# Attention values by seven block products instead of eight, one step behind the scores

## The reference

```python
q = (inputs_q @ Wq).reshape(b, sq, H, HD) * (1.0 / np.sqrt(HD))     # H = 16 heads of 128
k = (inputs_kv @ Wk).reshape(b, skv, H, HD)                         # skv = 12544, D = 512
v = (inputs_kv @ Wv).reshape(b, skv, H, HD)
scores = jnp.einsum('bqhd,bkhd->bhqk', q, k)
attn = jax.nn.softmax(scores, axis=-1)
ctx = jnp.einsum('bhqk,bkhd->bqhd', attn, v).reshape(b, sq, H * HD)
return ctx @ Wo
```

## Time and profile before

| | |
|---|---|
| median of 3 runs | 2128.65 us (2127.99 to 2130.28) |
| time of the profiled execution | 2126.51 us |
| its span, first to last instruction | 2124.7 us |
| mean granted PE clock | 0.988 |
| PE busy | 2053.5 us, 97% of the span |
| DVE busy | 1197.5 us, 56% |
| ACT busy | 914.0 us, 43% |
| POOL busy | 152.0 us, 7% |

### The profile page before, as it was taken

The page is one execution under the profiler, slowest core; times in us unless marked ns, Lnnn a source line. Parts: engine busy times, 40 slices in busy tenths (PEclk is TensorE's granted clock), DMA queues, the critical chain, the costliest instruction groups (busy, mean ns, idle before and its releaser), DMA issues.

```text
span 2124.7 us, 29323 instructions
## 1 busy us (share of the span) xinstructions
PE 2053.5 (97%) x11196; PEld 1107.3 (52%) x11200; DVE 1197.5 (56%) x2159; ACT 914.0 (43%) x1985; POOL 152.0 (7%) x209
## 2 busy tenths in 40 slices
PE   5899999999999999999999999999999999999886
PEld 4645555555555455555555555555555555555562
DVE  5665555455555556665666665555545555554426
ACT  4444445444444444344444444444444444443212
POOL 1000100000100101001001001010010010000001
PEclk8899999999999999999999999999999999999998
DMA  5424535444445344454545553443434333423660
GB/s 165 119 58 87 109 80 120 83 106 99 99 90 114 65 100 104 103 119 89 128 95 112 110 102 75 90 89 66 100 65 90 74 86 75 95 60 55 189 222 5
DMA packets 516699, 206.75 MB, mean 97 GB/s; under 512 B 418864, under 2 KB 502832, under 8 KB 515664
## 3 DMA queue, kind: packets, MB, share of 16 engines
q1 hardware_dynamic: 516560, 204.88, 43.6%
HBM read 97.59 MB, written 4.46 MB: 48 GB/s over the span
## 4 chain that ended last, share of the span: by engine, by line
PE 92%; DVE 4%; issue 1%; DMA 1%; ACT 1%; POOL 1%; SPq 0%; DVEq 0%; POOLq 0%; ACTq 0%
PE ps_s L1102 24%; PE ps_t L1102 18%; PE ps_c L1126 12%; PE ps_b L1126 12%; PE ps_a L1126 12%; PE ps_u L1126 12%; PE ps_b L1080 1%; PE ps_t L1184 1%; DVE bulk L775 1%; DMA bulk<-in_vo 0%; PE ps_s L1063 0%; PE ps_s L1227 0%; POOL stages L498 0%; DVE unt L909 0%; PE ps_u L1251 0%
## 5 line engine op out<-in xcount | busy, mean ns | idle before, releaser
L1102 PE MATMUL ps_s<-bulk 128*128 128x384 f16 (+2 forms) x3264 | 579.5, 321 | 27.1 <-DVE bulk L775 26.2
L1102 PE MATMUL ps_t<-bulk 128*128 128x384 f16 (+2 forms) x2448 | 449.3, 320 | 1.3 <-ACT ps_t L628 1.0
L1102 PEld LDWEIGHTS ps_s<-bulk 128*128 128x128 f16 x3264 | 315.2, 98 | 241.3 <-DVE bulk L775 29.2
L1102 PEld LDWEIGHTS ps_t<-bulk 128*128 128x128 f16 x2448 | 235.0, 98 | 151.1 <-ACT ps_t L628 1.9
L628 ACT ACTIVATE ps_t<-ps_s 128x384 f32<-128x384 f32 (+2 forms) x136 | 62.9, 462 | 502.6 <-PE ps_s L1102 502.6
L1126 PE MATMUL ps_u<-nring,pt 128*128 128x512 f16 x1194 | 269.1, 379 | 0.0
L1126 PE MATMUL ps_a<-nring,pt 128*128 128x512 f16 x1194 | 269.1, 379 | 0.0
L498 POOL TENSOR_TENSOR stages<-stages 128x256 f32<-128x256 f32 x196 | 143.6, 732 | 1683.3 <-DMA stages<-in_ctx 1664.1
L1126 PE MATMUL ps_b<-nring,pt 128*128 128x512 f16 x1158 | 260.7, 379 | 0.0
L1126 PE MATMUL ps_c<-nring,pt 128*128 128x512 f16 x1158 | 260.7, 379 | 0.0
L808 DVE SCALAR_TENSOR_TENSOR pp<-prob,pp 128x768 f16<-128x768 f32 (+2 forms) x272 | 239.0, 920 | 0.0
(11 more groups left out here) (197 smaller groups left out, 1556.3 us busy)
## 6 DMA issues: line engine op xcount, KB each, us to landing
stages<-in_ctx SPq DMA_DIRECT2D x392, 128.0 KB, 2.8
wst<-in_w SPq DMA_DIRECT2D x64, 256.0 KB, 3.3
bulk<-in_vo SPq DMA_DIRECT2D x16, 512.0 KB, 4.7
acc<-in_qk SPq DMA_DIRECT2D x12, 512.0 KB, 5.1
pt<-pp SPq DMA_TRANSPOSE x272, 4.0
tern_d<-wter SPq DMA_DIRECT2D x32, 128.0 KB, 3.1
bulk<-tern_d SPq DMA_DIRECT2D x2, 2048.0 KB, 10.7
wst<-in_qk SPq DMA_DIRECT2D x4, 512.0 KB, 5.6
```

The source lines that it names most:

```text
L1102: ins = mm(out, q_part(e, qlo, a)[:, c * P:(c + 1) * P], t_moving(k, tlo, b, c), start=(first and c == 0 and qlo == 0 and tlo == 0), stop= ...
```

## The change

The values are now also a 2 x 2 block product of seven block products: the rows are the two heads, the inner halves are the two halves of a chunk, and the outer halves are the two halves of the 512 columns. Each block product has matmuls of 256 columns, three for each chunk.

- POOL forms four sums of probability blocks (`S1` to `S4`, each 128 x 384 float32 at w = 3) for each step, after the exponentials (`sum_p`). It also forms the four context sums for the value layout now (`sum_t` for both kinds of chunk).
- ACT and DVE make high and low parts of seven blocks instead of four: one piece of three blocks (A22, A11, A12), then S1, S3, S2, S4 one by one. S2 and S4 are done at the start of the next step.
- SP transposes seven blocks of high and low parts in two DMAs, group 0 with A22, A11, A12, S1 and group 1 with S2, S3, S4. `pt` is single buffered.
- The values run one step behind the scores (`LAG = 1`), with the copies `value_a`, `value_e_u` on ACT and the additions `value_sums` on DVE between their products.
- The value layout of a context chunk grows from 1024 to 1792 columns, in high and low parts.
- Buffers share memory: `diff`, `mask`, `wg1`, `wg2` are loaded near the end, `x` is loaded again at the end, and the last attention weight `aw_o` is loaded together with `aw_k` and `aw_v` instead of after the last head.
- In the first eight steps the query parts are made one step earlier, and the queries and the new value products use the same PSUM.

```diff
-LAG = 2
+LAG = 1
...
-P_SCALE = 2.0 ** 15
+P_SCALE = 2.0 ** 14
...
             def turn_p(k, g):
-                sp.wait_ge(lo_done[g], k + 1)
-                if k >= LAG:
-                    sp.wait_ge(u_done[g], k - 1)
-                n = 4 * cols(k)
-                at = ((k % 2) * 2 + g) * 4 * WIN * P
-                sp.dma_start_transpose(pt[:, at:at + n].rearrange("p (t q) -> p t q", q=P),
-                                       pp[:, g * 2 * WIN * BLK:g * 2 * WIN * BLK + n]).then_inc(in_pt[g], 16)
+                sp.wait_ge(lo_done, 5 * k + (2, 5)[g])
+                if k:
+                    sp.wait_ge(v4_done, k)
+                at, n = p_at(k, g), (8, 6)[g] * cols(k)
+                sp.dma_start_transpose(pt[:, at:at + n].rearrange("p (t q) -> p t q", q=P), pp[:, at:at + n]).then_inc(in_pt[g], 16)
...
             sp.wait_ge(s4_done, NS)
             sp.dma_start(aw_q, aw_d[0]).then_inc(in_aw, 16)
             load_vo(4)
-            sp.wait_ge(u_done[1], NS)
-            for n, w in enumerate((aw_k, aw_v)):
+            sp.wait_ge(v4_done, NS)
+            for n, w in enumerate((aw_k, aw_v, aw_o)):
                 sp.dma_start(w, aw_d[n + 1]).then_inc(in_aw2[n], 16)
-                load_vo(5 + 2 * n)
-                load_vo(6 + 2 * n)
+                load_vo(5 + n)
+            sp.dma_start(xin, x_d).then_inc(in_xr, 16)
+            load_vo(8)
...
+            def sum_p(k):
+                for n, (dst, a, b, op) in enumerate(((S1, A21, A22, ALU.add), (S3, A11, A21, ALU.subtract),
+                                                     (S2, S1, A11, ALU.subtract), (S4, A12, S2, ALU.subtract))):
+                    if n == 0:
+                        pool.wait_ge(exp_done[0], k + 1)
...
+                    if n == 1:
+                        pool.wait_ge(exp_done[1], k + 1)
+                    if n >= 2:
+                        pool.wait_ge(p_sum, 4 * k + n - 1 + (n == 3))
+                    nc.gpsimd.tensor_tensor(prob_part(k, dst), prob_part(k, a), prob_part(k, b), op).then_inc(p_sum, 1)
...
+            for k in range(NS):
+                found = prep_at(k)
+                if found is not None:
+                    sum_t(found[0])
+                sum_p(k)
...
+            def value_a(k):
+                act.wait_ge(v1_done, k + 1)
+                if k:
+                    act.wait_ge(acc_done[0], k)
+                nc.scalar.activation(val_b, val_a, ACT.Copy).then_inc(va_copied, 1)
+
+            def value_e_u(k):
+                act.wait_ge(v5_done, k + 1)
...
+                nc.scalar.activation(part_e[:, 0:BLK], val_e, ACT.Copy).then_inc(ve_copied, 1)
+                act.wait_ge(v6_done, k + 1)
...
+                nc.scalar.activation(part_u[:, 0:BLK], val_b, ACT.Copy).then_inc(vu_copied, 1)
...
             def step(k):      
                 nc.scalar.activation(bank_b(k), bank_a(k), ACT.Copy).then_inc(a_copied, 1)
+                if k:
+                    hi_part(k - 1, S2, 1, 3)
                 act.wait_ge(s5_done, k + 1)
                 nc.scalar.activation(part_e[:, 0:cols(k)], bank_e(k), ACT.Copy).then_inc(e_copied, 1)
+                if k:
+                    hi_part(k - 1, S4, 1, 4)
...
+                if k:
+                    value_a(k - 1)
                 exp_head(k, 0)
+                if k:
+                    value_e_u(k - 1)
                 exp_head(k, 1)
...
+                hi_part(k, A22, 3, 0)
+                hi_part(k, S1, 1, 1)
+                hi_part(k, S3, 1, 2)
...
+            def value_sums(k):                             # DVE
+                v.wait_ge(v7_done, k + 1)
...
+                nc.vector.tensor_tensor(val_d, val_b, part_e[:, 0:BLK], ALU.add).then_inc(vd_done, 1)
+                v.wait_ge(v3_done, k + 1)
+                v.wait_ge(vu_copied, k + 1)
+                nc.vector.tensor_tensor(val_e, val_e, part_u[:, 0:BLK], ALU.add).then_inc(ve_done, 1)
...
             def step(k):                                   # DVE
+                if k:
+                    lo_part(k - 1, S2, 1, 4)
+                add_values(k - 2, 1)
+                if k:
+                    lo_part(k - 1, S4, 1, 5)
+                add_values(k - 2, 0)
...
+                if k:
+                    value_sums(k - 1)
+                lo_part(k, A22, 3, 1)
+                lo_part(k, S1, 1, 2)
+                lo_part(k, S3, 1, 3)
...
+            def value_product(k, dst, a, b, first, last):
+                for n in range(w):
...
+                    for plo, clo in ((0, 0), (0, 1), (1, 0)):
+                        tile = p_at(k, g, plo, a % PURE) + n * P
+                        ins = mm(dst, pt[:, tile:tile + P], n_part(c, clo, b), start=(first and n == 0 and plo == 0 and clo == 0),
+                                 stop=(last and n == w - 1 and plo == 1), skip_group_check=True)
...
+            def values(k):
+                pe.wait_ge(in_pt[0], 16 * (k + 1))
...
+                if k:
+                    pe.wait_ge(acc_done[0], k)
+                    pe.wait_ge(acc_done[1], k)
...
+                value_product(k, val_a, A11, B11, True, False).then_inc(v1_done, 1)
...
+                value_product(k, val_e, S1, T1, True, False).then_inc(v5_done, 1)
+                pe.wait_ge(in_pt[1], 16 * (k + 1))
+                pe.wait_ge(va_copied, k + 1)
+                value_product(k, val_b, S2, T2, False, False).then_inc(v6_done, 1)
+                value_product(k, val_a, A12, B21, False, True)
+                pe.wait_ge(vu_copied, k + 1)
+                value_product(k, val_b, S3, T3, False, False).then_inc(v7_done, 1)
+                pe.wait_ge(ve_copied, k + 1)
+                value_product(k, val_e, S4, B22, False, True).then_inc(v3_done, 1)
+                pe.wait_ge(vd_done, k + 1)
+                value_product(k, val_b, A22, T4, False, True).then_inc(v4_done, 1)
```

More of the change, by code:

```diff
@@ L176, in perceiver_layer @@
         b2b, nwb = wst[:, 0:D], wst[:, D:2 * D]
-        aw_k, aw_v = (nring[:, n * KC * D:(n + 1) * KC * D] for n in range(2))
-        aw_o = unt[:, :]
+        aw_k, aw_v, aw_o = (nring[:, n * KC * D:(n + 1) * KC * D] for n in range(3))
+        xin, x1 = (nring[:, 3 * KC * D + n * D:3 * KC * D + (n + 1) * D] for n in range(2))
+        xin0, y0 = (pt[:, n * 2 * D:(n + 1) * 2 * D].bitcast(F32) for n in range(2))
         decay = stages[:, 0:AH * P]
+        late = stages[:, 8 * BLK:16 * BLK]
+        diff, mask, g1t, wg1 = (late[:, n * P:(n + 1) * P] for n in range(4))
+        wg2 = late[:, 4 * P:4 * P + D]
         xt = x2
@@ L590, in split_hi @@
                     return
[L591 removed]
+                j, kind, c = found
+                act.wait_ge(t_sum, 4 * (j + 1))
                 if kind == 0:
[L593 removed]
                     dst = t_ring(c, 0)
@@ L1132, in step @@
-            def step(k, between=None):
+            def value_product(k, dst, a, b, first, last):
+                _, lowest, w = STEPS[k]
+                g = a // PURE
+                for n in range(w):
+                    c = next(c for c in range(lowest, lowest + w) if ring_slot(c) == window(k)[4][n])
+                    for plo, clo in ((0, 0), (0, 1), (1, 0)):
+                        tile = p_at(k, g, plo, a % PURE) + n * P
+                        ins = mm(dst, pt[:, tile:tile + P], n_part(c, clo, b), start=(first and n == 0 and plo == 0 and clo == 0),
+                                 stop=(last and n == w - 1 and plo == 1), skip_group_check=True)
+                return ins
@@ L1133, in step @@
+            def step(k):
                 _, a, w = STEPS[k]
@@ L1153, in step @@
                 if ii < NP:
-                    q_prime(2 * ii + 1)
+                    q_prime(2 * ii)
                 pe.wait_ge(d_done, k + 1)
                 product(k, bank_b(k), A22, T4, False, True).then_inc(s4_done, 1)
-                for g, n in chunks(k - LAG):
-                    values(k - LAG, g, n)
+                if ii < NP:
+                    q_prime(2 * ii + 1)
+                if k:
+                    values(k - 1)
             for ii in range(2):
@@ L1165, in _ @@
                 step(k)
-            for g, n in chunks(NS - 2):
-                values(NS - 2, g, n)
             def turn(f):
@@ L1196, in _ @@
             finish(0)
-            for g, n in chunks(NS - 1):
-                values(NS - 1, g, n)
+            values(NS - 1)
             for f in range(1, H):
```

342 lines of the change are left out of this document (177 added, 165 removed).

## The result

The changed kernel takes **2346.18 us** (median of 4 runs, 2340.97 to 2353.77) against 2128.34 (4 runs): ratio 1.1033, 95% interval 1.1012 to 1.1053. It is 218 us slower; 2281 had been predicted, with 2145 to 2340 as the range, so the result lies 6 us above the range. The profiled execution took 2340.97 us, of which 2339.2 are its span.

What follows compares the result with a forecast made beforehand. PE was taken to bound the kernel before, the loop through the transposes after the change. 123 x (15.85 - 14.61) = +153 us, with start and end 0, on 2126.5 gave 2279.5, so 2281 us as median; range 2145 to 2340.

Steps and rivals of the forecast that it cites:

- PE work: Value products on PE: 6.93 us per step instead of 7.77, 13.75 in all; 106 us back if nothing waited.
- The loop: Chain from third value product through additions, low parts and two transposes to the next step's: 14.9 us without a conflict.
- Y: Start of the third value product (S2 T2) in a step, from which the loop's times are counted.
- The conflict: POOL's probability sums and DVE's low parts take turns: first transpose issued 0.95 us later, mean period 15.85 us.
- The start: First eight steps: gain of at most 36 us of idle PE against at most 24 of DVE work, taken as 0.
- The steps: Steps 8 to 130: 123 x (15.85 - 14.61) = +153 us.
- The end: Five short steps and last values, 0 within 5 us; tail with one more 1 MB load, 0 to 6, taken as 0.
- DVE goes first twice: Rival: DVE's two low parts run before POOL's sum S4; period 14.9 to 15.0 us, 2172 us, chance 0.18.
- Large transposes run faster: Rival: transposes cost less per tile than 0.155 us; no change at 0.125, 2023 us at 0.095 or less; chance 0.12.
- The conflict spreads: Rival: POOL's context sums block low parts of S2 and S4, group 1 issued late; period 16.35, 2343 us, chance 0.12.
- The chain is shorter: Rival: pieces of the loop overlap, so PE binds; 2023 to 2120 us, chance 0.08.

Runs made afterwards that it cites:

- half_lag2_clear: half_lag2 with GpSimd's probability and context sums also cut to 2 columns each: 2040.0 us, ratio 0.9594 to the kernel before.
- pool_narrow: Changed kernel with GpSimd's four probability sums writing 2 columns of each block from step 9 on: 2296.0 us, ratio 1.0790 to the kernel before.
- half_tiles: Changed kernel with only the high parts' tiles transposed in steps 9 to 130 (12 and 9 tiles): 2185.8 us, ratio 1.0266 to the kernel before.
- pe_reduce: Changed kernel with the weight scales' sum over partitions made by a 2-column matmul on PE instead of GpSimd: 2340.6 us, ratio 1.1005 to the kernel before.
- sums_clear: pool_narrow with GpSimd's context sums also cut to 2 columns: 2222.8 us, ratio 1.0462 to the kernel before.
- half_lag2: Changed kernel with low parts' tiles never transposed and values two steps behind the scores again: 2178.5 us, ratio 1.0244 to the kernel before.

## Why the prediction was right in sign and too small

**PE work.** Right: 13.75 us per step was predicted, half_lag2_clear shows 13.70, 0.91 less than before. The gain of some 110 us is real and lies under the rest.

**The loop.** Right, step by step. Predicted: issue at Y + 7.35 to 7.55, both landed 8.4 later, period 15.75 to 15.95. Measured: issue 7.25, landed 8.44 in the median, the median step 15.70. One detail differs: the long low part hardly had to wait for S2, which ended at Y + 4.50, as DVE came (it lasts 1.43 us in the mean, 1.35 alone), so the wait that the prediction called certain was nearly absent. The two transposes follow each other in SP's queue: the second is issued 3.76 us after the first, when SP is through with that one's 24 tiles, and its source was ready 0.7 us before (low part of S4 done at 1024.41, issue at 1025.1). The two waits of PE are 0.76 and 0.57 us, where over 1 and about 1 were named; a third, 0.39 us per step for DVE's addition of the scores, adds to them and was not foreseen; with it PE idles 1.8 us per step, not over 2.

**The conflict.** Right in kind (whole instructions, taking turns) and nearly in size: 0.82 us per step where 0.95 was charged. The Trainium skill's rule (SBUF — State Buffer, Who interferes with whom) agrees with the trace on all three points that it has: the shared port is held for a whole instruction, low parts are 557 ns alone and 928 beside POOL, and additions with one PSUM input stay at 432. What it doesn't say, who is next, the trace shows as turns without an exception: in steps 8 to 130 GpSimd issued 560 sums while a low part or a context split was running, and each ended 0.59 us (256 columns) or 0.86 us (384) after that instruction's end, within 0.01, so none waited for a second one.

**Where the 65 us are.** The miss is 24.8 at the start (taken as 0), 13.9 at the end (0), 22.8 in the steps (175.8 against 153), and 3 us by which the median lies further above the profiled execution than before.
- *The start was the largest error*, and it is the step "I take 0" that failed: a gain of at most 36 us was set against a loss of at most 24 on DVE. The 36 were read wrong. They are the idle time of PE from 0, and 12 of them lie ahead of the first scores, where there is no step yet. From 24.40 on the kernel before has
```profile
24.40:141.10 116.70, 93.04 (x650) 67.55 (x651) 77.13 (x123) 53.90 (x98) 12.82 (x16) 0.90 0.42 106
PE ps_s L1102 <- DVE bulk L775: 26.2, 8, 7.0
```
  The wait in the second line, for the low parts of the queries, did go away (2.7 us are left), but waits came in its place that the prediction had not named. The largest in the changed kernel:
```profile
PE ps_w L1175 <- DVE acc L907: 12.2, 4, 4.2
PE ps_w L1212 <- DVE ps_w L914: 8.9, 5, 2.4
PE ps_t L1199 <- ACT ps_t L685: 8.2, 5, 3.7
```
  The first is of the queries, which must wait until DVE has added up values, since both use the same PSUM. Together PE idles 35.7 us there instead of 23.7, which is +12.0, and works 105.8 instead of 93.0, which is +12.8. Part of this work is only moved: with LAG = 1 the values of one more step, 63 matmuls or 6.9 us, are done ahead of step 8.
  Three other traces with the same start but for two instructions at most (pool_narrow, half_tiles, pe_reduce) have step 8 at 168.5 to 168.6. sums_clear begins it at 158.0, so POOL's sums on the port cost 8 to 10 us there; with lag 2 and half the tiles as well (half_lag2_clear) it is 150.1. The 9 us that remain against 141.1 are 3.5 of PE work and 5.5 of idle PE; what each change added to them was not tried.
- *The steps*: 123 x (15.70 - 15.85) = -18; the partition sum's stall, 26.96 - 15.70 = +11; and some +30 from steps longer than the median. In those the second transpose lands up to 10.3 us after the first issue. It goes with packets in the queues that the profile names "instruction". The DMA rows of such a step, 1596.3 to 1606.7 us in 40 slices, have one packet of 16 KB in q8; it begins at 1602.8 us and takes 0.94, and at its end (slices 29 to 31) nearly all 16 DMA engines stand idle:
```profile
DMA  0000299999999999998899999996000299989973
q8 instruction: 1, 0.02, 0.6%
```
  Over steps 9 to 130 the split is clean. In 69 steps no packet of an instruction queue meets the transposes, and both have landed 8.38 us after the first issue in the mean, 8.47 at most. In 53 steps one does, and it is 9.04 in the mean: 53 x 0.66 = 35 us, enough for the +30. Without such a packet none of 89 second transposes took over 4.72 us; with one of 16 KB in its midst it takes 0.7 to 1.9 us more. pool_narrow, sums_clear and pe_reduce show the same split; no run moved the packets, so that they are the cause rests on this coincidence and not on an experiment.
- *The end* was put at 0 too. The lines of the stretches have it in the last one, 152.4 us instead of 136.9, with 7.8 us more PE work and 7.7 more idle PE; what makes them was not tried.

**The rivals.** "DVE goes first twice" is out: its 14.9 to 15.0 is what a kernel with hardly any conflict has (sums_clear, median step 14.81). "Large transposes run faster" is out at 0.156 us a tile. While they run, all 16 DMA engines are busy; the DMA rows of the changed kernel, 1612 to 1621 us, in 40 slices:
```profile
DMA  0000000000000000059999999999999999999999
GB/s 0 0 0 0 0 0 0 0 0 0 0 0 0 0 0 0 0 123 228 216 210 208 221 213 223 213 222 216 221 215 220 213 160 171 244 218 206 217 215 216
```
Some 215 GB/s; the 261 GB/s of the Trainium skill (DMA: Bandwidth & Descriptors, Latency and other measured facts) were not reached by the transposes of the runs here. "The conflict spreads" gave 2343 us, 3 from the result, and is wrong all the same: its mechanism, a low part of S4 too late for the queue, is not in the trace. This low part was done at least 0.54 us ahead of the second issue in each of the 122 steps. That the time of this rival came so near is luck. "The chain is shorter" is out, as PE idles 222 / 123 = 1.8 us per step.

**What no rival had.** Even with the loop open and half the tiles the change brings nothing: half_lag2 is at 2179 us. There are two limits above PE's 13.7 us, each shown with the other taken away, and with both away (half_lag2_clear) the period is 13.77: the loop through the transposes, 15.2 us, and DVE's queue with the port in it, 14.8. I had checked DVE by its sum, 11.2 us per step, and found it under 13.75; with the waits for the port it is 1531 / 123 = 12.4, in steps that prepare a chunk more, and its instructions stand in a fixed order.

## What to carry to other kernels

Ask of each stage not only how busy an engine is, but which chain must close within one period: a result that is used one step later instead of two turns slack into a loop, and here its transposes alone are 8.4 of 16 us. When work goes to GpSimd because it is idle, count what it does to each VectorE instruction with two SBUF inputs, and let sums that nobody needs yet wait on a semaphore until the urgent instruction is through (69 us here by one wait). Two bounds of opposite sign don't make a zero: the start, costed that way, was over a third of the miss. And before idle time is counted as something to gain, look at where in its stretch it lies.

## What the runs showed of the hardware that I had not expected

- A wait for the shared port is recorded as the instruction's own duration: a 384-column low part of 0.55 us shows as 1.35, GpSimd's 384-column sum of 1.00 (by itself, at 129.26 us) as 2.11. DVE's busy time fell by 244 us with not one instruction fewer.
- GpSimd's partition reduction shows as 0.41 us but keeps the engine away for 13.1 us; the kernel before has 7.7 us of the same behind it, which nothing noticed, as GpSimd had nothing else to do.
- Taking work off GpSimd can move the conflict instead of ending it: pool_narrow's freed time was filled by the next sums in its queue, which hit the same instructions of VectorE.
- A packet of 16 KB in a queue that the profile calls "instruction" takes about 1 us, and a transpose of 18 tiles in whose midst it falls lands 0.7 to 1.9 us later than the 4.65 us of the others. In the kernel before, whose transposes are used 1.5 steps later, PE idles for 2 us in all 123 steps.
